# A graph layer with two aggregated planes: ScalarE exchanges the halves of one plane, VectorE adds it to the other, and TensorE makes one product a tile, two ticks later

## The reference

```python
h  = relu(layernorm(x))
a0 = segment_sum(edge_attr_64 @ W_edge.T, dst) / clip(degree, 1)      # mean over a node's edges
x  = x + concat([h @ W_self.T, a0 @ W_neigh.T]) @ W_final.T + b_final
h  = relu(layernorm(x))
a1 = segment_sum(edge_attr_128, dst)
x  = x + relu(concat([h, a1]) @ W1 + b1) @ W2 + b2
```

## Time and profile before

| | |
|---|---|
| median of 3 runs | 577.51 us (575.9 to 578.47) |
| the profiled execution, its own time | 575.72 us |
| its span, first to last instruction | 573.9 us |
| TensorE (matmul) busy | 514.9 us |
| VectorE busy | 408.5 us |
| GpSimd busy | 361.1 us |
| ScalarE busy | 152.5 us |
| mean granted TensorE clock | 0.966 |
| moved by DMA | 169.53 MB |

### The profile page before, as it was taken

The page is one execution under the profiler, slowest core; times in us unless marked ns, Lnnn a source line. Parts: engine busy times, 40 slices in busy tenths (PEclk is TensorE's granted clock), DMA queues, the critical chain, the costliest instruction groups (busy, mean ns, idle before and its releaser), DMA issues.

```text
span 573.9 us, 26023 instructions
## 1 busy us (share of the span) xinstructions
PE 514.9 (90%) x11043; PEld 459.6 (80%) x11043; DVE 408.5 (71%) x1166; ACT 152.5 (27%) x353; POOL 361.1 (63%) x524
## 2 busy tenths in 40 slices
PE   7869688899799999899998998989999979999993
PEld 6858677788788888778887897879888868988782
DVE  4555888775777878787887688768877866867421
ACT  0012012341223332432234224223322522222201
POOL 1737746778376774675767776674974773775630
PEclk9878999999989999999999999999999989999997
DMA  8946999999979999999999998988999986978920
GB/s 288 365 135 216 376 375 319 330 328 317 311 235 316 341 320 313 313 305 303 319 317 328 314 345 295 359 274 287 342 328 327 344 263 209 378 263 283 354 69 11
DMA packets 113228, 169.53 MB, mean 295 GB/s; under 512 B 5486, under 2 KB 84310, under 8 KB 113111
## 3 DMA queue, kind: packets, MB, share of 16 engines
q1 hardware_dynamic: 85843, 154.42, 77.9%
q10 hardware_dynamic: 27268, 13.43, 8.1%
HBM read 161.43 MB, written 6.40 MB: 292 GB/s over the span
## 4 chain that ended last, share of the span: by engine, by line
PE 58%; DVE 26%; issue 8%; DVEq 4%; DMA 1%; POOL 1%; SPq 1%; ACT 0%; ACTq 0%; POOLq 0%
PE ps L630 19%; PE ps L648 11%; DVE onehot L1010 8%; PE ps L693 7%; DVE agg L1039 7%; PE ps L632 4%; PE ps L706 3%; PE ps L714 3%; PE ps L677 3%; PE ps L668 3%; PE ps L707 2%; DVEq L1039 2%; DVE bn L1082 2%; DVEq L1017 2%; DVE bn L1127 1%
## 5 line engine op out<-in xcount | busy, mean ns | idle before, releaser
L521 POOL TENSOR_TENSOR hot_part<-onehot 128x384 bf16<-128x384 f32 (+2 forms) x128 | 112.5, 879 | 177.9 <-DVE onehot L1010 167.6
L630 PE MATMUL ps<-onehot,ring 128*64 128x64 f32 x3126 | 216.4, 227 | 8.9 <-issue 8.9
L632 PE MATMUL ps<-onehot,ring 128*64 128x64 f32 x3126 | 216.8, 227 | 8.4 <-issue 8.2
L630 PEld LDWEIGHTS ps<-onehot,ring 128*64 128x64 f32 x3126 | 197.4, 140 | 32.1 <-issue 27.3
L632 PEld LDWEIGHTS ps<-onehot,ring 128*64 128x64 f32 x3126 | 197.5, 140 | 7.5 <-issue 7.5
L1039 DVE TENSOR_TENSOR agg<-ps,agg 128x128 f32 (+1 forms) x319 | 97.2, 305 | 131.4 <-PE ps L657 59.1
L1010 DVE TENSOR_TENSOR onehot<-iota_win,rel 128x768 f32<-128x768 f32 (+2 forms) x128 | 150.9, 1180 | 0.4
L648 PE MATMUL ps<-onehot,ring 128*64 128x64 f32 x3126 | 119.1, 224 | 2.5 <-issue 2.5
L648 PEld LDWEIGHTS ps<-onehot,ring 128*64 128x64 f32 x3126 | 107.0, 139 | 7.5 <-issue 7.1
L693 PE MATMUL ps<-w_c,agg 128*128 128x129 f32 x424 | 55.9, 287 | 8.4 <-DVE agg L1039 5.9
L693 PEld LDWEIGHTS ps<-w_c,agg 128*128 128x128 f32 x424 | 52.2, 199 | 13.2 <-DVE agg L1039 7.0
(11 more groups left out here) (118 smaller groups left out, 590.9 us busy)
## 6 DMA issues: line engine op xcount, KB each, us to landing
ring<-in_edge_attr_dram SPq DMA_DIRECT2D x95, 768.0 KB, 5.3
ring<-in_edge_attr_dram SPq DMA_DIRECT2D x96, 384.0 KB, 7.0
ring<-in_edge_attr_dram SPq DMA_DIRECT2D x32, 832.0 KB, 5.4
ring<-in_edge_attr_dram SPq DMA_DIRECT2D x32, 416.0 KB, 7.4
x<-in_x_dram ACTq DMA_DIRECT2D x23, 256.0 KB, 6.1
out_dram<-x ACTq DMA_DIRECT2D x23, 256.0 KB
x<-in_dst_dram SPq DMA_DIRECT2D x1, 384.0 KB
x<-in_dst_dram SPq DMA_DIRECT2D x1, 208.0 KB, 3.4
```

What stands on the lines that cost most here:

```text
L521: nc.gpsimd.tensor_tensor(out, a, b, ALU.add).then_inc(s_hotsum, 1)
L630: nc.tensor.matmul(bank[0:H, o:o + WIN], ring128[0:K, slot, u, 0:H], hots, start=u == 0, stop=r == R - 1, skip_group_check=True)
L632: nc.tensor.matmul(bank[H:P, o:o + WIN], ring128[0:K, slot, u, H:D], hots, start=u == 0, stop=r == R - 1, skip_group_check=True)
```

## The change

22 of the 25 groups are "merged": all but the two with two sets of columns and the last one. For them:

- ScalarE, at tick `TAKE` and as the last thing of its tick, copies plane 2 of the group into a new tile `swapped`, the upper 64 partitions to the lower ones and the lower ones to the upper, two copies of 64x512 (`swap`). It waits for what `neigh` waited for before.
- VectorE, at tick `TAKE` + 1, adds `swapped` into plane 1 of `agg` (`merge`, 128x512).
- TensorE makes one product for each tile instead of two, at tick `NEIGH` = `TAKE` + 2, and waits for `s_merged`.
- Everything of these groups that had a distance from `TAKE` has the same distance from `NEIGH`, so it stands two ticks later. `SELF` goes with it. The first `SELF` is 6 instead of 4.

For the other three groups nothing changes but the distances of q = 22 and 23, which also move by two; the last stays at 128. The diff, cut to its core (the other hunks put `NEIGH` for `TAKE` in the tick distances listed above):

```diff
+    MERGED = [q for q, g in enumerate(SEQ[:-1]) if g not in BOTH]
+    NEIGH = [t + 2 if q < NG - 1 else t for q, t in enumerate(TAKE)]
...
-        t = min(TAKE[q] - 9, SELF[0] - 2 if SELF else CH)
+        t = min(NEIGH[q] - 9, SELF[0] - 2 if SELF else CH)
...
+        swapped = sb("swapped", [P, GW])
...
             def neigh(q):
                 g = SEQ[q]
-                pe.wait_ge(s_added, ADDED[min(CH, TAKE[q])])
-                for i, (k, _) in enumerate(FOLDS):
-                    if k == q:
-                        pe.wait_ge(s_fold, 2 * i + 2)
+                if q in MERGED:
+                    pe.wait_ge(s_merged, MERGED.index(q) + 1)
+                else:
...
-                parts = [(a, k) for a in columns_of(g) for k in range(2)]
+                parts = [(a, k) for a in columns_of(g) for k in range(1 if q in MERGED else 2)]
...
+            def swap(m):
+                q = MERGED[m]
+                (a,), w = columns_of(SEQ[q]), tiles_of(SEQ[q]) * P
+                act.wait_ge(s_added, ADDED[min(CH, TAKE[q])])
+                for i, (k, _) in enumerate(FOLDS):
+                    if k == q:
+                        act.wait_ge(s_fold, 2 * i + 2)
+                if m:
+                    act.wait_ge(s_merged, m)
+                nc.scalar.copy(swapped[0:H, 0:w], agg[H:P, 2, a:a + w])
+                nc.scalar.copy(swapped[H:P, 0:w], agg[0:H, 2, a:a + w]).then_inc(s_swap, 1)
...
+            def merge(m):
+                q = MERGED[m]
+                (a,), w = columns_of(SEQ[q]), tiles_of(SEQ[q]) * P
+                dve.wait_ge(s_swap, m + 1)
+                nc.vector.tensor_tensor(agg[:, 1, a:a + w], swapped[:, 0:w], agg[:, 1, a:a + w], ALU.add).then_inc(s_merged, 1)
...
             for t in range(TICKS):
                 for q in range(NG):
+                    if t == NEIGH[q] + 1:
+                        layer_0(q)
...
+                for m, q in enumerate(MERGED):
                     if t == TAKE[q] + 1:
-                        layer_0(q)
...
+                        merge(m)
```

More of the change, by code:

```diff
@@ L169, in bounds @@
             hi = lo
-            while hi + 1 in LOWER and hi + 1 in free and (hi < 4 or TAKE[TURN[hi - 3]] + 11 <= t):
+            while hi + 1 in LOWER and hi + 1 in free and (hi < 4 or NEIGH[TURN[hi - 3]] + 11 <= t):
                 hi += 1
@@ L178, in bounds @@
         lo = hi
-        while lo - 1 in UPPER and lo - 1 in free and (lo - 1 > NG - 5 or TAKE[TURN[lo + 3]] + 11 <= t):
+        while lo - 1 in UPPER and lo - 1 in free and (lo - 1 > NG - 5 or NEIGH[TURN[lo + 3]] + 11 <= t):
             lo -= 1
@@ L200, in build_gnn @@
     for q in range(NG - 1, -1, -1):
-        t = min(TAKE[q] - 9, SELF[0] - 2 if SELF else CH)
-        while any(t + 4 == r + 6 or t + 6 == r + 10 for r in TAKE):
+        t = min(NEIGH[q] - 9, SELF[0] - 2 if SELF else CH)
+        while any(t + 4 == r + 6 or t + 6 == r + 10 for r in NEIGH):
             t -= 1
@@ L501, in clear @@
             def clear(k, a, b):
-                done = [q for q in range(NG) if TAKE[q] + 9 == k]
+                done = [q for q in range(NG) if NEIGH[q] + 9 == k]
                 if done:
@@ L731, in _ @@
                 for q in range(NG):
[L732 removed]
+                    if t == NEIGH[q]:
                         neigh(q)
[L734 removed]
+                    if t == NEIGH[q] + 8:
                         hidden(q)
[L736 removed]
+                    if t == NEIGH[q] + 10:
                         output(q)
@@ L944, in _ @@
                         norm_1(q)
+                for m, q in enumerate(MERGED):
+                    if t == TAKE[q]:
+                        swap(m)
             def general():
@@ L1177, in _ @@
                 for q in range(NG):
-                    if t == TAKE[q] + 1:
-                        layer_0(q)
-                    if t == TAKE[q] + 11:
-                        result(q)
-                    if t == TAKE[q] + 2:
-                        stats_2(q)
-                    if t == TAKE[q] + 4:
-                        scale_2(q)
+                    if t == NEIGH[q] + 1:
+                        layer_0(q)
+                    if t == NEIGH[q] + 11:
+                        result(q)
+                    if t == NEIGH[q] + 2:
+                        stats_2(q)
+                    if t == NEIGH[q] + 4:
+                        scale_2(q)
+                for m, q in enumerate(MERGED):
+                    if t == TAKE[q] + 1:
+                        merge(m)
                 for q in range(NG):
```

31 lines of the change are left out of this document (16 added, 15 removed).

## The result

The median went from 576.70 us (574.54 to 578.47, four runs beside it) to 584.75 us (582.81 to 588.55, four runs), a ratio of 1.0192 with a 95% interval of 1.0148 to 1.0236. A repetition (`e5_after_again`) gave 1.0153 [1.0108, 1.0198]. The prediction said 570 and a range of 561 to 583: it named the wrong sign. The profiled execution took 583.46 us.

What follows compares the result with a forecast made beforehand. TensorE was taken to bound the first stretch, VectorE the second, both nearly full in the third. Changes of -3.6, +1.2 and -5.0 us summed to -7.4: 568.3 us for the profiled execution, 570 for the median, range 561 to 583.

Steps and rivals of the forecast that it cites:

- VectorE's merge: One added 128x512 add a merged group on VectorE: 0.65 us each on the path, bounds 0.45 and 1.4.
- The second rival: SBUF port shared with GpSimd makes VectorE the bound; merges cost 1.2 to 1.4 us, 582 us at 1.3; chance 0.24.
- M: The price of one merge on VectorE's path in us, taken as 0.65.
- ScalarE: Two added 64x512 copies a group on ScalarE, 1.2 us a group, counted as costing the kernel nothing.
- TensorE's product: TensorE's product at line 693: 176 fewer records, busy near 33 us, 0.9 us less a group, 19.8 us in all.
- First stretch: TensorE bounds; 4 x 0.9 = 3.6 us gained: From 83 to 145 us: four groups' relief counts in full, and four merges, 2.6 us, fit in VectorE's 7.2 us of waits.
- second and third: 145 to 305 us: 4.0 us of waits back, 5.2 lost; 305 to 500 us: 9.0 to 13.9 back, 6.5 lost.
- 18M - 19.05: Total change of time in us by price of a merge: zero at 1.06 us a merge, 2.9 us faster at 0.90.
- So I count no new wait there: TensorE's wait for the merge: the tightest place found, at tick 99, holds with 0.6 us to spare.
- No idle time of 3 us before the product of q = 4: TensorE's 3.12 us wait there for VectorE's fold would go, and VectorE's 2.42 us wait for the next sums with it.
- if the clock falls in new places because TensorE now idles more often: Condition named beforehand, without a size, under which the prediction would be wrong: new drops of TensorE's granted clock.
- Start and end: The kernel outside the three middle stretches, before 83 us and after 500 us: no change of time.

Runs made afterwards that it cites:

- e5_after_again: The changed kernel unaltered, measured again beside the kernel before: 1.0153 of the kernel before.
- the own product apart: Changed kernel, with the own product also barred from the tick of another group's result in the same PSUM bank: 1.0022, repeated 0.9999, of the kernel before.
- the first pair: Two kernels without copies or merges, groups two ticks later, own product as it was: with both products 0.9951, with one 0.9909 of the kernel before.
- e2: Changed kernel with copies and merges, but both products kept, plane 2 counted twice: 584.68 us, 1.0134 of the kernel before.
- e1: Kernel before with the groups two ticks later, both products kept, no copies, no merge: 571.72 us, 0.9951 of the kernel before.
- e3: Changed kernel without copies and merges, one product a tile, second plane left out: 569.87 us, 0.9909 of the kernel before.
- e10: Kernel before moved two ticks later, both products, own product also barred from the tick of another group's result: 1.0014 of the kernel before.
- e7: Changed kernel without ScalarE's copies; VectorE adds plane 2 as it stands, halves not exchanged: 1.0147 of the kernel before.
- e6: Changed kernel with ScalarE's copies but without VectorE's merge, plane 2 left out: 0.9921 of the kernel before.

## Why the prediction was wrong

**VectorE's merge: right in size, in part by luck.** I took 0.9 us a record and 0.65 on the path, between 0.45 and 1.4. The trace has 0.856, and taking merges out gives 0.59 to 0.74 each. But that price holds waits of TensorE that I hadn't counted: with the own product apart it is 0.42 to 0.48, just at my lower bound. The lock stretches some, not each. The second rival, M of 1.2 to 1.4, gave a time close to what came (582), for a reason that isn't there.

**ScalarE: right.** Two copies of 0.617 us; the merge never waited for them, and without them nothing changes.

**TensorE's product: right in size.** 176 records fewer, 34.8 us busy against 33 foretold.

**The step that failed: "First stretch: TensorE bounds; 4 x 0.9 = 3.6 us gained", and with it the gains of 4.0 and 9.0 to 13.9 us in the second and third.** By my formula 18M - 19.05 a free merge would have given 19 us (M = 0); the shift and one product together gave 0.0091, 5.2 us, of which the relief has 2.4. I had read 91 to 94% of TensorE's busy time, and a chain full of its lines, as TensorE being the bound, so that its time comes off the end. But a chain that runs through TensorE says only that the step before was TensorE's, not that the next step could come earlier. TensorE is tied to VectorE at every tick through three PSUM banks and at `ps_row`; a faster TensorE arrives earlier at `result` and stands there longer (15.0 us against 11.3). A second part went into no wait that names an engine: TensorE's idle time without a releaser was 7.7 us longer with one product than with two (11.0 with the own product apart), and in the first pair its clock was lower (below). I had put these at nothing. They are read from single executions, so how the 17 us that are missing divide between them stays open.

**"So I count no new wait there", and the shift at nothing.** I looked for waits only at the merge's own successor, and listed no other pair of instructions in which one engine frees what the other needs. The table forbids the own product in the tick of another group's `output` (`t + 6 == r + 10`), but not one tick later, where `result` frees the bank. The shift made no new pairs of this kind, since own parts and results move together: by the tables ten own products stand in such a tick before the change and nine after it. What changed is how late VectorE is there, and how early TensorE. Before the change three of them waited, 3.3 us, and I had no row of them. After it six wait, 19.5 us, the largest wait of TensorE with a named releaser. The shift alone makes it 11.3 us; with TensorE's relief it is 15.0, with the merges but both products (`e2`) 10.6, and with both 19.5. So it takes the relief and the later VectorE together. The one condition that takes it away gives back 7 to 11 us, as much as the loss of 9. But it moves thirteen own parts and brings a wait of 14.0 us at the `output`, so it shows that the places of the own parts decide over these us, not that this wait alone does.

**"No idle time of 3 us before the product of q = 4": wrong.** It is still there, as `PE ps L701 <- DVE agg L1134`, 4.2 us in two waits, the longest 3.1: two ticks later the product waits for the merge instead of the fold.

**The clock.** I had written that it would prove me wrong "if the clock falls in new places because TensorE now idles more often". It did: a mean of 0.935 over the four runs (0.962 for the kernel before), and windows at 0.62. Over 104 timed runs of the kernel before, each 0.01 of mean clock goes with 1.6 us of time (correlation -0.51, so not all of the scatter; 2.0 us if ten longer ones are taken in). By that slope 0.027 is 4 us of the 8 to 9, and the fall from 0.958 to 0.943 between `e1` and `e3` some 2 us of the relief. This is an estimate from a slope among runs of one program; no experiment held the clock.

**Start and end: "nothing".** The start grew by some 3 us. It can't be the merges, as the first of them stands behind the sums of tick 13; the shift alone has a start of 83.3 and 85.2 us (`e1`, `e10`) where the kernel before has 81.3 and 82.5, each in one execution. The first group's own part, now at tick 6, is what moved there; that it is the cause is not shown. Behind tick 113 the time grew by 3.6 us, where no merge stands any more (the last starts at 486.0 us). The shift alone has 75.5 there, the changed kernel 78.6 and 77.1, one product without merges 80.7 to 82.7, and behind 485 us TensorE's idle time without a releaser is 1.8 us with the shift, 4.1 in the changed kernel and 5.4 in `e3`. Neither end was tried by itself.

**The sum, in measured parts** (us, from the ratios): shift -2.8, relief -2.4, copies 0, merges +14 to +16, together the measured +9 to +11. This sum closes by construction, since the merges' price is the changed kernel less the one without them; with the price that `e7` and `e6` give by themselves, 13.0, it is +7.8. I had foretold 0 for the shift, -19 for the relief and the waits that it would free, 0 for the copies, and +14.3. The price came near what I computed; the relief didn't.

## What to carry to other kernels

An engine that is 92% busy and fills the chain is not yet a bound whose relief comes off the end: ask for each instruction behind the relieved one what it waits for, and how late that is. Where every engine's place is a table of ticks, list the pairs that share a buffer (here one PSUM bank, `ps_row`) and check each pair's distance against how far the freeing engine lags, not only the pair that the change is about. A distance that stays the same can become too short when one engine gets work and the other loses it. Before a difference of 1 or 2% is put down to a change, compare the idle time without a releaser in both traces: here it alone differed by up to 15 us between kernels. A trade between two engines near balance pays only if the dearer one keeps its slack: here 10 us of relief at best stood against 10 us of price.

## What I had not expected of the hardware

- Two-input VectorE adds of 128x512 from SBUF take 0.656 us at least, 0.786 in the median and 1.749 at most; the longest end 0.55 us behind a GpSimd instruction that had started before them. A reduction of the same 512 columns, with one SBUF input, took 0.651 to 0.684 in all 22 cases.
- Three waits of TensorE of 3.6 to 4.4 us were followed by its lower clock for several microseconds: the 1.06 us product took 2.04. Freeing TensorE went with a lower mean granted clock in one pair of kernels (0.958 to 0.943), but not with the own product apart (0.954 and 0.957).
- Idle time within TensorE's sums with no releaser in the trace was 9.4 us in one program and 20.4 in another with the same instructions in half of the span; their times differ by 2%. Nine in ten of the longer stops, over all traces, end 2.2 to 2.6 us behind the start of a 16 KB packet of the DMA queue `instruction`.
